# Rotary and causal attention stage: two blocks are transposed and copied ahead of the next tile's scores, other work goes behind the first products

## The reference, cut to what matters

```
x = x + gb * ffn(...)                     # the experts' rows, gathered and added, 8 a token
h = layernorm(x) * (1 + ca) + sa
xh = h.reshape(Bx, Tx, d, N_HEADS)
q, k, v = (einsum('btqh,qdh->btdh', xh, w).reshape(Bx, Tx, Dx) for w in (w_q, w_k, w_v))
q, k = _rope(q), _rope(k)
scores = einsum('bqd,bkd->bqk', q, k) / sqrt(Dx)      # one head of width 256
scores = where(causal, scores, -inf)
x = x + ga * (softmax(scores) @ v)
```

## Time and profile before

| what | us |
|---|---|
| median of 3 runs | 5782.2 (5778.06 to 5784.22) |
| the profiled execution | 5784.91 |
| its span on the core | 5783.2 |
| this stage, from its first `scores` to its last output | 815 (3741.2 to 4556.3) |

### The profile page before, as it was taken

How to read it: one execution, slowest core, us unless ns; L and a number is a source line. 1 busy time by engine, 2 the same in 40 slices (tenths; PEclk the granted TensorE clock), 3 DMA queues, 4 the chain that set the end, 5 groups by cost and what they waited for, 6 DMA issues and landing times. The chain is left out here.

```text
span 5783.2 us, 106990 instructions
## 1 busy us (share of the span) xinstructions
PE 4961.7 (86%) x37182; PEld 2607.9 (45%) x37184; DVE 4323.1 (75%) x5246; ACT 3136.3 (54%) x5403; POOL 938.3 (16%) x886
## 2 busy tenths in 40 slices
PE   6589999999999999999932758467999879999998
PEld 3233333333333333333322336235666647677676
DVE  4589999999999999999466223466665557777777
ACT  1068888888888888888921212112222234444443
POOL 0000000000000000000007720443220013334333
PEclk8689999999999999999965879778999969999998
DMA  5322333323322222222111047421110120100000
GB/s 180 109 93 91 100 100 97 98 88 98 103 91 81 77 82 81 82 80 78 32 43 66 14 128 235 147 76 58 54 37 1 59 73 22 26 23 22 26 23 14
DMA packets 241629, 431.82 MB, mean 75 GB/s; under 512 B 37945, under 2 KB 142410, under 8 KB 239008
## 3 DMA queue, kind: packets, MB, share of 16 engines
q1 hardware_dynamic: 197424, 355.18, 19.9%
q0 software_dynamic: 26928, 62.99, 3.4%
q10 hardware_dynamic: 16896, 8.39, 0.6%
HBM read 329.36 MB, written 133.89 MB: 80 GB/s over the span
## 5 line engine op out<-in xcount | busy, mean ns | idle before, releaser
L579 DVE TENSOR_REDUCE attn_mpart<-attn_ps_max 128x2 f32<-128x1024 f32 x2048 | 2498.6, 1225 | 122.6 <-PE attn_ps_max L617 111.1
L524 ACT ACTIVATE attn_probs<-attn_ps_exp 128x512 f32<-128x512 f32 x4096 | 2222.0, 595 | 350.8 <-PE attn_ps_exp L633 103.5
L617 PE MATMUL attn_ps_max<-attn_keys,attn_quer 54*128 54x512 f32 x4096 | 1503.5, 462 | 82.2 <-DMA attn_keys<-k_laid 55.1
L633 PE MATMUL attn_ps_exp<-attn_quer,attn_keys 54*128 54x512 f32 x4096 | 1505.9, 450 | 23.6 <-issue 13.5
L648 PE MATMUL attn_ps_out<-attn_probs,attn_vals 128*32 128x256 f32 x16384 | 1317.7, 393 | 8.4 <-ACT attn_o_sb L530 7.8
L633 PEld LDWEIGHTS attn_ps_exp<-attn_quer,attn_keys 54*128 54x128 f32 x4096 | 615.1, 186 | 877.1 <-ACT attn_probs L524 839.6
L648 PEld LDWEIGHTS attn_ps_out<-attn_probs,attn_vals 128*32 128x32 f32 x16384 | 324.0, 108 | 755.8 <-issue 400.5
L617 PEld LDWEIGHTS attn_ps_max<-attn_keys,attn_quer 54*128 54x128 f32 x4096 | 602.6, 190 | 123.4 <-DVE attn_mpart L579 63.5
L1442 PE MATMUL ra_psO<-ra_vals,ra_probT 128*128 128x256 f32 x1152 | 299.7, 410 | 80.2 <-DVE ra_probT L1614 80.0
L1371 POOL DMA_INDIRECT ra_rows<-y_rows,slots x256 | 253.8, 991 | 379.6 <-DVE ra_total L1536 308.2
L1500 ACT ACTIVATE ra_row<-ra_psS 128x512 f32<-128x512 f32 x112 | 66.9, 597 | 448.7 <-PE ra_psS L1423 448.7
(11 more groups left out here) (324 smaller groups left out, 6001.5 us busy)
## 6 DMA issues: line engine op xcount, KB each, us to landing
attn_keys<-k_laid SPq DMA_DIRECT2D x256, 304.0 KB
attn_vals<-v_aug SPq DMA_DIRECT2D x128, 512.0 KB, 15.0
attn_keys<-k_laid SPq DMA_DIRECT2D x256, 128.0 KB
x_rows<-attn_zeros POOLq DMA_DIRECT2D x16, 1280.0 KB, 9.9
exp_x<-x_rows SPq DMA_DIRECT2D x64, 320.0 KB
exp_w1w<-in_w SPq DMA_DIRECT2D x64, 256.0 KB
y_rows<-exp_y SPq DMA_DIRECT2D x64, 256.0 KB
q_laid<-proj_parts SPq DMA_DIRECT2D x32, 256.0 KB
```

What stands on the lines that cost most here:

```text
L524: act.activation(probs[k % 2][:, j, :], ps_exp[bank_of(g, n)][:, :], ACT.Exp).then_inc(exp_done, 1)
L579: dve.tensor_reduce(mpart[i][:, kb, TC * pair + tile::TC * NPR], ps_max[u % 2][:, :, :], AX, ALU.max).then_inc(unit_read, 1)
L617: mm = pe.matmul(ps_max[u % 2][:, h, :], quer[g][half(h), pair, tile * P:(tile + 1) * P], keys[g % 2][half(h), pair, kb * CH:(kb + 1) * CH ...
L633: pe.matmul(ps_exp[bank_of(g, n)][:, :], keys[g % 2][half(h), pair, k * P:(k + 1) * P], quer[g][half(h), pair, :], start=True, stop=True). ...
```

## The change

Three lists are put in another order; no instruction is added, dropped or resized. On PE tile s now begins with `turn(s, 0)` and `turn(s, 1)`, and so with the wait for `exps(s)`; then come `scores(s + 1)` and `products(s, 0)`; `turn_h` and `values` stand behind `products(s, 0)`, and `heads(c, n)` behind `products(s, n + 1)` (before, behind `products(s, n)`). On DVE `copy_probs(s, 0)` and `(s, 1)` stand ahead of `sum_rows`, `statistics`, `normalise` and `maximum(s + 1)`, and `rotate(c, n)` moves with `heads(c, n)`. On ACT `exps(s + 1)` stands ahead of `copy_h` and `copy_v`.

```diff
--- before.py
+++ after.py
@@ -1445,24 +1445,26 @@
 
                 def tile(s):
                     c, j, nb = following(s), s % TC, blocks(s)
-                    if s + 1 < NT:
-                        scores(s + 1)
-                    if c is not None and j == 2:
-                        turn_h(c)
-                    if c is not None and j == 3:
-                        values(c)
                     pe.wait_ge(exped, s + 1)
                     if s >= 2:
                         pe.wait_ge(o_read, s - 1)
-                    turn(s, 0)
+                    for b in range(min(2, nb)):
+                        turn(s, b)
+                    if s + 1 < NT:
+                        scores(s + 1)
                     for b in range(nb):
-                        if b + 1 < nb:
+                        if b and b + 1 < nb:
                             turn(s, b + 1)
                         products(s, b)
-                        if c is not None and j == 2 and b < NAB:
-                            heads(c, b)
+                        if c is not None and j == 2:
+                            if b == 0:
+                                turn_h(c)
+                            elif b <= NAB:
+                                heads(c, b - 1)
+                        if c is not None and j == 3 and b == 0:
+                            values(c)
                     if c is not None and j == 2:
-                        for n in range(nb, NAB):
+                        for n in range(nb - 1, NAB):
                             heads(c, n)
 
                 pe.wait_ge(w_loaded, 16)
@@ -1519,12 +1521,12 @@
                         copies(s + 1)
                     if c is not None and j == 1:
                         sqrt_chunk(act, norm_step, NORM_STEPS * c, rstd)
+                    if s + 1 < NT:
+                        exps(s + 1)
                     if c is not None and j == 2:
                         copy_h(c)
                     if c is not None and j == 3:
                         copy_v(c)
-                    if s + 1 < NT:
-                        exps(s + 1)
 
             @block.vector
             def _(dve):
@@ -1623,6 +1625,8 @@
 
                 def tile(s):
                     c, j, nb = following(s), s % TC, blocks(s)
+                    for b in range(min(2, nb)):
+                        copy_probs(s, b)
                     if s + AHEAD1 < NT:
                         sum_rows(s + AHEAD1)
                     if c is not None and j == 1:
@@ -1631,14 +1635,13 @@
                         normalise(c)
                     if s + 1 < NT:
                         maximum(s + 1)
-                    copy_probs(s, 0)
                     for b in range(nb):
-                        if b + 1 < nb:
+                        if b and b + 1 < nb:
                             copy_probs(s, b + 1)
-                        if c is not None and j == 2 and b < NAB:
-                            rotate(c, b)
+                        if c is not None and j == 2 and 1 <= b <= NAB:
+                            rotate(c, b - 1)
                     if c is not None and j == 2:
-                        for n in range(nb, NAB):
+                        for n in range(nb - 1, NAB):
                             rotate(c, n)
                     add_output(s)
```

## The result

The changed kernel takes 5707.6 us, median of 4 runs (5697.9 to 5721.3); the kernel before, on the same chip, 5780.1 (5775.4 to 5784.2). The ratio is 0.9882, 95% interval 0.9867 to 0.9896. The profiled execution took 5707.3 us, its span 5705.6. The stage shrank from 815.1 to 744.4 us, 70.7 less; its start also lies 2.5 us earlier in this trace, which is the scatter of what runs ahead of it.

The account below looks back on a forecast made before the run. The prediction took late PE itself, and early a loop through DVE, as the bounds. Chunk gains of 2.4 to 12.6 us sum to 66.3: 5784.9 - 66.3 = 5718.6 profiled, 5716 for a median; range 5698 to 5743.

Parts of the forecast that it names:

- Plain late tiles: Plain tiles of seven or eight blocks: PE's wait for probT goes and nothing new is late; gain 1.63 us each.
- two-block loop: Early plain tiles of two blocks: exponential, turns, copies, sum, maximum, exponential take 10.3 us, with statistics 12.3.
- Slow for the first group behind a wait over 3 us: PE's clock in new early tiles: assumed slow for one group; half rate throughout 18 us less gain, full rate 8 more.
- The sign named for this part: In the profile after, PE would wait on the exponential (L1433) for 1 to 4 us in tiles 1 to 9.
- The tiles with j = 2: Head-preparing tiles: mixed; PE newly waits for copy_h behind the exponential, 5.2 us in tile 22, a slow group (1.8) behind.
- (b): Cost of the new wait before heads(c, 0): nothing to 5.2 + 1.8 us in each of seven tiles; sum holds 14 + 7.
- Gathers (1): Rival: gathers bound the early tiles, all at 1.89 + 0.30 us; gain 43, time 5739; chance 0.07.
- The clock staying low (2): Rival: PE's clock stays low in the early tiles; gain 48 us, time 5734; chance 0.10.
- The slower case (3): Rival: waits in j = 2 tiles hold PE at 1.2 GHz for the tile's rest, about +100 us, 5816; chance 0.03.
- Little happening (4): Rival: little happens, since the copies were hidden already; chance 0.01.

Follow-up runs that it names:

- turns_ahead_again: Against the kernel before, only two turns and their copies go ahead of the scores; head work, values and ACT's order stay old: stage 733.7 us.
- pad_after: Changed kernel with about 1.4 us of extra DVE work (two additions) ahead of each row maximum: stage 775.4 us.
- act_back_again: Changed kernel with ACT's copy_h and copy_v ahead of exps(s + 1) again, second taking on another chip: stage 729.4 us, ratio 0.9842; first taking 0.9901.
- norm_first: Changed kernel with normalise ahead of sum_rows on DVE in the j = 2 tiles: stage 752.1 us.
- after_again: The changed kernel itself, unaltered, measured once more on another chip: 5712.9 us, ratio 0.9883 to the kernel before.
- norm_first_act_back: Changed kernel with normalise ahead of sum_rows and ACT's copy_h and copy_v ahead of the exponential again: stage 717.5 us, whole time 5684.7 us.
- early_only: Changed kernel's order in tiles 0 to 15 only, the old order in tiles 16 to 31: stage 770.7 us.

## Why the prediction was right

**The forecast.** 5716 for 5707.6 measured; 66.3 us of gain in the stage for 70.7. The mechanism was the one named: behind the change late tiles are PE alone and early ones a loop through DVE. turns_ahead_again shows that the turns and copies ahead carry it, pad_after shows which tiles are the loop. Chunk by chunk, predicted and measured: 63.1 and 63.9, 63.9 and 63.9, 71.7 and 71.4, 80.9 and 81.0, 96.3 and 94.7, 108.8 and 107.2, 119.4 and 118.6, 144.7 and 143.7. That the early chunks agree so well is in part luck. In chunk 1, to the digit, the four tiles were to take 10.5, 10.3, 12.3 and 30.8 us and took 11.6, 10.1, 13.3 and 29.0.

**Plain late tiles.** 1.63 us each was too little: the tile went from 29.1 to 27.2. Idle time in the profile starts at the modelled end of the last matmul; from start to start (4323.00 to 4325.67 in the earlier trace rows, 2.67) less the 0.88 that two turns take without a wait (4246.77 to 4247.65) the loss was 1.79, and the products behind it took 0.1 longer. From `scores(31)` to the last output it is 50.9 us (53.6 before) for a predicted 52.1, and 30.7 from `scores(28)` to `scores(29)` for a predicted 30.0: I had put the turns ahead into the wrong tile, which cancels but for 0.5.

**Early tiles.** The two-block loop was to be 10.3 us and is 10.1 to 10.3; tile 9 was to be 15.6 with its third copy 3 us late, and is 15.0 with 3.11 of wait, but without the slow group; tile 12, 15.7 and 15.5; tile 13, 17.3 and 17.3. "Slow for the first group behind a wait over 3 us" held well enough for a sum (the turns and scores behind the 3.23 wait in tile 4 took 6.05 from start to start against about 4.3 at full rate), but it is too simple: behind 3.11 us in tile 9 hardly anything was slow in this run (1.99 for 1.89), and all of it in act_back_again. The sign named for this part was a wait for the exponential of 1 to 4 us in tiles 1 to 9; it is 5.3 and 5.0 in tiles 1 and 2, 3.2, 0.6, 4.5 and 1.4 in tiles 4, 5, 6 and 8, and none in 3, 7 and 9. (The products in the earlier trace rows end at 3858.4, not at 3858.3; nothing rests on it.)

**The tiles with j = 2.** The wait for `hT` was to be 4.8, 5.2, 1.9 and 2.5 us in tiles 18, 22, 26 and 14, and was 4.25, 4.93, 1.50 and 1.56; a slow group stands behind it in 18 and 22, hardly in 26 and 14 (1.12 and 1.13 for 1.02). Tile 2, which I had not named, has a wait of 1.46. My sum for these tiles was still too long, by 2.3 in tile 18 and 1.9 in tile 22 (36.1 and 37.7 for 38.4 and 39.6): I had added 0.9 for two turns ahead to a figure that held them already, and missed the same 0.8 in the tiles with j = 3. (For tile 22 the working even ends at 39.3, and the sum has 39.6; no row gives the 0.3.) Of (b), 14 us of wait and 7 of slow clock in the sum, act_back_again gives 15.0 back: the waits were sized right (13.7 inside the stage), the slow clock too high. What I did not ask was whether this part of the change is worth having: it isn't, in ACT's part.

**Rivals.** Gathers (1) end a wait of DVE twice, 2.5 us together; POOL's 256 gathers took 253.8 us before and 255.0 after, so a tighter DVE list does not slow them, though single ones of 1.89 us are still there. The Trainium skill (SBUF — State Buffer, "SBUF: two separate sides") states that GpSimd can't write the descriptors of a DMA while VectorE runs an instruction in a 2-port perf mode. No run here shows which instructions of VectorE, if any, ran in that mode. The clock staying low (2) is refuted by chunks 1 and 2 at 0.89 and 0.95 and by the products of tile 4 at full rate. The slower case (3) needed 16 us of slow work a tile; in tile 22 the second head was at full rate again. Little happening (4) is refuted by tile 24 and by the 70.7 us.

## What to carry to other kernels

When one engine feeds another through a copy, put the copy ahead of the long reductions of the next tile in both lists, and, where tiles are short, give the producer as many blocks ahead as it has buffers (two here); here that is worth 81 us of 815, and the second block 19 in the changed kernel. Before an instruction is moved behind another on an in-order engine, follow what that other one waits for: `copy_h` behind `exps` put PE behind DVE's maximum and cost 15 us, and made a good edit (`normalise` first) a bad one. Judge an edit with the other in place and without it, for their effects don't add: +7.6 and -15.0 alone, -26.9 together.

## What the runs showed that was not expected

- Slow work behind a wait costs only where nothing else would have held PE. In tile 6 `turn_h` and a block of products behind 3.21 us took 1.97 and 2.73 us for 1.04 and 1.89, and `hT` came no later for it; in norm_first four half heads behind 4.97 us took 2.08, 1.91, 2.07 and 1.91 for 1.02, and all of it was lost. Whether the length of the wait or its place made them so slow was not tested.
- What a wait costs behind its end is not a function of its length. In tile 9 PE waits 3.08 to 3.11 us in seven runs in which the tile's order is the same, and the next eight records take 1.99 us at a granted clock of 1.00 (after, after_again, norm_first), 2.50 at 0.77 (norm_first_act_back), 3.37 and 3.40 at 0.58 (early_only, turns_ahead_again) and 3.78 at 0.50 (act_back_again). Waits of 1.42 to 1.97 us right before products cost these 0.1, and in the kernel before all those from 3.5 us up were followed by 3.78. What decides between them stays open. Tile 9 as a whole takes 15.0 to 17.6 us in these runs, so a sum for such a tile can't be better than that.
- The same program ran 2.8% longer on one of the chips. The profiled execution of act_back is 205 us longer there than that of act_back_again: 167 lie ahead of this stage and 36 in it, where single engines stand still at places that no row explains. No run was made to find the cause; it stays open.
